# Graph-masked attention on one core: batches without a loop, and four places in the schedule moved

## The reference

```python
h = jnp.maximum(_layernorm(x, axis=-1), 0.0)
q = (h @ Wq + bq).reshape(b, n, H, HD)      # k and v in the same way
scores = jnp.einsum('bihd,bjhd->bhij', q, k) / jnp.sqrt(jnp.float32(HD))
scores = scores + jnp.where(adj == 0, -1e9, 0.0)[None, None, :, :]
weights = jax.nn.softmax(scores, axis=-1)
x = x + jnp.einsum('bhij,bjhd->bihd', weights, v).reshape(b, n, H * HD)
```

## Time and profile before

| | before |
|---|---|
| median of 3 runs | 4096.61 us (4095.68 to 4096.75) |
| the profiled execution | 4094.8 us, span of its instructions 4093.0 us |
| granted TensorE clock | 0.996 of full speed |
| busy: PE | 4027.1 us (98%) |
| busy: DVE, ACT, POOL | 76%, 75%, 34% |

### The profile page before, as it was taken

How to read it: one execution, slowest core, us unless ns; L and a number is a source line. 1 busy time by engine, 2 the same in 40 slices (tenths; PEclk the granted TensorE clock), 3 DMA queues, 4 the chain that set the end, 5 groups by cost and what they waited for, 6 DMA issues and landing times.

```text
span 4093.0 us, 77408 instructions
## 1 busy us (share of the span) xinstructions
PE 4027.1 (98%) x22016; PEld 3279.4 (80%) x22016; DVE 3100.4 (76%) x5128; ACT 3075.5 (75%) x5514; POOL 1394.2 (34%) x1409
## 2 busy tenths in 40 slices
PE   7999999999999999999999999999999999999998
PEld 6888888878887888878888788887888878888886
DVE  6877878777777777768777687776877868778686
ACT  5877868778686786867868688686886868868687
POOL 4333333333333333323333333332333333333322
PEclk9999999999999999999999999999999999999999
DMA  5232322322222222223222232222322323223121
GB/s 181 69 92 63 85 65 77 86 66 83 80 64 84 72 82 81 62 80 84 70 81 70 73 91 62 81 80 63 92 65 77 84 57 92 77 65 92 44 73 47
DMA packets 240106, 316.30 MB, mean 77 GB/s; under 512 B 16400, under 2 KB 147472, under 8 KB 231056
## 3 DMA queue, kind: packets, MB, share of 16 engines
q1 hardware_dynamic: 239632, 310.71, 26.6%
HBM read 172.23 MB, written 37.75 MB: 51 GB/s over the span
## 4 chain that ended last, share of the span: by engine, by line
PE 81%; issue 9%; POOL 5%; DMA 2%; ACT 2%; SPq 1%; DVE 0%; POOLq 0%; ACTq 0%; DVEq 0%
PE T L559 18%; PE misc L517 14%; PE S L547 10%; PE S L548 10%; PE O L571 10%; PE O L578 10%; PE misc L530 8%; DMA xln<-in_x 1%; POOL kB L400 1%; POOL kA L400 1%; PE misc L587 1%; PE misc L496 1%; POOL xln L381 1%; ACT y L670 1%; POOL outs L420 1%
## 5 line engine op out<-in xcount | busy, mean ns | idle before, releaser
L847 DVE TENSOR_TENSOR pT<-T,pT 128x512 fp32r<-128x512 f32 x2048 | 1390.7, 688 | 712.5 <-ACT pT L679 699.7
L679 ACT CAST pT<-T 128x512 fp32r<-128x512 f32 x2048 | 1185.5, 590 | 671.1 <-PE T L559 573.6
L841 DVE CUSTOM_DVE_ANT_0 S<-S,mask 128x1024 f32<-128x1024 f32 x1024 | 1257.2, 1228 | 9.0 <-PE S L548 8.1
L559 PE MATMUL T<-ident,probs 128*128 128x128 f32 x8192 | 1233.9, 273 | 0.6 <-DVE pT L847 0.2
L559 PEld LDWEIGHTS T<-ident,probs 128*128 128x128 f32 x8192 | 1005.1, 140 | 279.7 <-DVE pT L847 36.4
L687 ACT ACTIVATE probs<-S,negmax 128x1024 f32<-128x1024 f32 x1024 | 1151.6, 1125 | 8.3 <-DVE negmax L841 5.1
L578 PE MATMUL O<-pT,vs 128*64 128x512 f32 x2048 | 965.6, 471 | 0.2 <-DVE pT L847 0.2
L571 PE MATMUL O<-pT,vs 128*128 128x512 f32 x2048 | 816.9, 399 | 14.7 <-issue 14.6
L517 PE MATMUL misc<-hT,wqk 128*128 128x512 f32 x3036 | 789.7, 395 | 4.3 <-ACT y L670 0.8
L517 PEld LDWEIGHTS misc<-hT,wqk 128*128 128x128 f32 x3036 | 557.0, 188 | 156.5 <-ACT y L670 18.4
L420 POOL TENSOR_TENSOR outs<-outs,oT 64x512 f32<-64x512 f32 x256 | 331.7, 1296 | 560.8 <-DMA outs<-oT 539.7
(11 more groups left out here) (70 smaller groups left out, 3590.3 us busy)
## 6 DMA issues: line engine op xcount, KB each, us to landing
wqk<-wqk_split SPq DMA_DIRECT2D x63, 1024.0 KB, 6.5
xln<-in_x SPq DMA_DIRECT2D x240, 256.0 KB, 2.6
outs<-in_x SPq DMA_DIRECT2D x66, 512.0 KB, 4.5
kA<-kA SPq DMA_DIRECT2D x128, 256.0 KB, 3.2
kB<-kB SPq DMA_DIRECT2D x128, 256.0 KB, 3.9
outs<-oT SPq DMA_DIRECT2D x256, 128.0 KB, 3.4
out<-outs SPq DMA_DIRECT2D x64, 512.0 KB, 4.0
probs<-in_adj SPq DMA_DIRECT2D x4, 1024.0 KB, 5.0
```

Source lines behind the costliest of these rows:

```text
L559: mm = pe.transpose(T[:, u % 2, i * P:(i + 1) * P], probs[:, (GB * g + i) % RING, j * P:(j + 1) * P], ident[:])
L679: act.copy(pT[:, u % PT, 0, :], T[:, u % 2, :]).then_inc(p_hi, 1)
L841: dve.tensor_tensor_reduce(S[:, s % 2, :], S[:, s % 2, :], mask[:, s % NB, :], 1.0, 3.0e38, ALU.add, ALU.min, negmax[:, s % RING:s % RING ...
L847: dve.tensor_tensor(pT[:, u % PT, 1, :], T[:, u % 2, :], pT[:, u % PT, 0, :].bitcast(F32), ALU.subtract).then_inc(p_lo, 1)
```

## The change

There are four parts.
1. The loop is gone: every batch is written out on every engine, with constant counts. The semaphore increments dve_passed, gp_passed and sp_passed go with it.
2. The second q/k chunk moves from units (5, 6) to (6, 7) of a pair, and the low parts of q are given units of their own (LOW_AT).
3. On SP the load of an x tile stands ahead of copy_k in the same unit, and the second copy_k moves from unit 15 to 16 of a pair.
4. In the units 122, 124, 126 and 0 TensorE scores only the first half of the block; the second half comes in the odd unit after it, ahead of V. VectorE's shift moves to that odd unit.

```diff
-QK_SLOTS = ((3, 4), (5, 6), (8, 9), (11, 12))
+QK_SLOTS = ((3, 4), (6, 7), (8, 9), (11, 12))
...
-LOW_AFTER = (1, 3)
+LOW_AT = {8: (1, 0), 10: (1, 1), 11: (2, 0), 13: (2, 1)}
...
-COPY_K_AT, STORE_AT, RES_AT, WQK_AT = (8, 15), 19, 24, (21, 21, 28, 21)
+COPY_K_AT, STORE_AT, RES_AT, WQK_AT = (8, 16), 19, 24, (21, 21, 28, 21)
...
+HALVED = (122, 124, 126, 0)
...
-                    for half in range(2):
-                        if v == COPY_K_AT[half] and not (last and p == PAIRS - 1):
-                            copy_k(b, p + 1, half)
                     if u in HT_AT and HT_AT[u] + XLN < NB and not last:
                         t = HT_AT[u]
                         sp.wait_ge(h_turned, NB * (b + 1) + t + 1)
                         load_xln(b + 1, t + XLN)
+                    for half in range(2):
+                        if v == COPY_K_AT[half] and not (last and p == PAIRS - 1):
+                            copy_k(b, p + 1, half)
...
-            with sp.Fori(0, B // 2 - 1) as two:
-                body(2 * two + 1)
-                body(2 * two + 2)
+            for b in range(1, B - 1):
+                body(b)
...
-            def score(b, s):
+            def score(b, s, halves=(0, 1)):
...
-                for half in range(2):
+                for half in halves:
...
-                mm.then_inc(scored, 1)
+                if 1 in halves:
+                    mm.then_inc(scored, 1)
...
-                if u % 2 == 0 and s < SBLOCKS:
-                    score(b, s)
-                if u % 2 == 0 and s >= SBLOCKS and not last:
-                    score(b + 1, s - SBLOCKS)
+                halves = (u % 2,) if u // 2 * 2 in HALVED else (0, 1) if u % 2 == 0 else ()
+                if halves and s < SBLOCKS:
+                    score(b, s, halves)
+                if halves and s >= SBLOCKS and not last:
+                    score(b + 1, s - SBLOCKS, halves)
...
-                    if u % 2 == 0 and s < SBLOCKS:
+                    due = u % 2 == (1 if u // 2 * 2 in HALVED else 0)
+                    if due and s < SBLOCKS:
                         shift(b, s)
...
-                    for second in range(2):
-                        v = u - LOW_AFTER[second]
-                        if v in QK_AT and QK_AT[v][1] in Q_CHUNKS and not (last and QK_AT[v][0] == PAIRS - 1):
-                            low_q(b, QK_AT[v][0] + 1, QK_AT[v][1], second)
+                    if u % PER in LOW_AT and not (last and u // PER == PAIRS - 1):
+                        low_q(b, u // PER + 1, *LOW_AT[u % PER])
```

More of the change, by code:

```diff
@@ L177, in adj_preln_kernel @@
         o_turned, y_scaled, y_added = sem("o_turned"), sem("y_scaled"), sem("y_added")
-        dve_passed, gp_passed, sp_passed = sem("dve_passed"), sem("gp_passed"), sem("sp_passed")
         block = ctx.enter_context(nc.Block())
@@ L219, in load_xln @@
             def load_xln(b, t):
-                sp.sem_inc(sp_passed)
                 sp.dma_start(xln[:, t % XLN, :], x[b, t * P:(t + 1) * P, :]).then_inc(xln_in[t % XLN], 16)
             def load_xres(b, p):
-                sp.sem_inc(sp_passed)
                 src = x[b].rearrange("(i t) c -> t i c", t=P)[:, :, p * P:(p + 1) * P]
@@ L364, in spread @@
                 gp.wait_ge(mv_done, n + tiles)
-                gp.sem_inc(gp_passed)
                 gp.tensor_scalar(rstd[:, ts], mv[:, ts, 1], EPS, None, ALU.add).then_inc(ln_part, tiles)
@@ L478, in _ @@
             body(0, first=True)
-            with gp.Fori(0, B // 2 - 1) as two:
-                body(2 * two + 1)
-                body(2 * two + 2)
+            for b in range(1, B - 1):
+                body(b)
             body(B - 1, last=True)
@@ L539, in score @@
                 pair = PAIRS * b + s // 16
[L540 to L543, removed]
-                for half in range(2):
+                if 0 in halves:
+                    pe.wait_ge(q_low, 4 * pair + 3 + (s // 8) % 2)
+                    pe.wait_ge(k_copied, 64 * (pair + 1))
+                    if some(n - 1):
+                        pe.wait_ge(exped, n - 1)
+                for half in halves:
                     cols = slice(half * HALF, (half + 1) * HALF)
@@ L644, in _ @@
             body(0, first=True)
-            with pe.Fori(0, B // 2 - 1) as two:
-                body(2 * two + 1)
-                body(2 * two + 2)
+            for b in range(1, B - 1):
+                body(b)
             body(B - 1, last=True)
@@ L787, in _ @@
             body(0, first=True)
-            with act.Fori(0, B // 2 - 1) as two:
-                body(2 * two + 1)
-                body(2 * two + 2)
+            for b in range(1, B - 1):
+                body(b)
             body(B - 1, last=True)
@@ L806, in stats @@
                 dve.wait_ge(bn_done, n + 1)
-                dve.sem_inc(dve_passed)
                 dve.bn_aggr(mv[:, t, :], bn[:, r, :]).then_inc(mv_done, 1)
@@ L907, in body @@
                     s = u // 2 + LEAD
-                    if u % 2 == 0 and s < SBLOCKS:
+                    due = u % 2 == (1 if u // 2 * 2 in HALVED else 0)
+                    if due and s < SBLOCKS:
                         shift(b, s)
-                    if u % 2 == 0 and s >= SBLOCKS and not last:
+                    if due and s >= SBLOCKS and not last:
                         shift(b + 1, s - SBLOCKS)
@@ L921, in _ @@
             body(0, first=True)
-            with dve.Fori(0, B // 2 - 1) as two:
-                body(2 * two + 1)
-                body(2 * two + 2)
+            for b in range(1, B - 1):
+                body(b)
             body(B - 1, last=True)
```

## The result

The changed kernel takes 4112.09 us (median of 7 runs, 4110.31 to 4113.07) against 4096.61 us (7 runs, 4093.86 to 4097.57). The ratio is 1.0039, 95% interval 1.0027 to 1.0051: slower by 0.39%, 15.5 us, where 8.8 us less were forecast.

What follows compares the result with a forecast made beforehand. The prediction took TensorE, busy 98% of the span, as the bound, so only its waits could change. Its terms summed to -8.8 us, taking the median from 4096.6 to 4087.8 us, range 4076 to 4098.

Steps and rivals of the forecast that it cites:

- Part 2, unit 11: a new wait: Unit 11: qB moved to unit 9 delays ScalarE's copy_y, so chunk 3 waits 0.75 us, 62 times: +46.5 us.
- unit 11 costs less: Rival: the moved qB copy overlaps its neighbours (4073 us) or is hidden wholly (4041 us); chance 0.14.
- the bound that took no overlap: ScalarE, units 9 and 10: qB's copy and probs_hi overlap no neighbour, so probs_hi moves by 0.76 us.
- the six branches: Batch passages, unit 127 to unit 2: the branches back cost 4.1 us each and go, -24.8 us.
- waits that stay: Unit 3 of three pairs and unit 77: waits grow by 0.06 us without the loop in 14 batches, +3.4 us.
- x tile 3, unit 85: Unit 85: TensorE's wait for the tile's normalisation goes in 15 batches because its load is issued earlier, -12.7 us.
- V next to V: Units 125, 127 and 1: halved scores between consecutive V remove 0.22 us each, in 15 batches, -9.9 us.
- unit 5: Chunk 1 no longer starts right after chunk 0, so 63 waits of 0.18 us go, -11.3 us.
- Part 1, no loop: Batch passages take 12.03 us without a branch instead of 16.34: -24.8 us, with +3.4 us from waits that grow.
- a straight stream that runs dry: Rival: instruction fetch stalls TensorE 2.4 us each time; one in each of 14 batches gives 4121 us; chance 0.10.
- small waits: With the rival that the early load fails or a later tile waits, they leave 4092 to 4101 us; chance 0.12.

Runs made afterwards that it cites:

- a1_low12: The changed kernel with q's low part (2, 1) on VectorE back in unit 12 instead of 13: 4092.61 us, ratio 0.9991 to the kernel before.
- a2_qb8: The changed kernel with chunk 1's second high part (qB) on ScalarE in unit 8, right behind the first, instead of the end of unit 9: 4055.92 us.
- a3_swap: The changed kernel with chunk 1's halves exchanged: upper-partition qB made in unit 8, lower-partition qA at the end of unit 9: 4087.22 us.
- b1_noloop: The kernel before with only the loop removed, all batches written out: 4067.66 us, ratio 0.9938.
- b2_xload: The kernel before with only the x tile load put ahead of the copies of k and the second copy_k in unit 16: 4082.65 us, ratio 0.9968.
- b3_halves: The kernel before with only the scores halved next to V: 4083.39 us, ratio 0.9971.
- b4_qk: The kernel before, loop kept, with only chunk 1 moved to units 6 and 7 and the low parts' new table: 4150.06 us, ratio 1.0136.
- d2_low9: The changed kernel with copy_y ahead of the exponential, qB high in unit 8, low parts in units 8, 9, 11, 12: 4045.04 us, ratio 0.9882.
- d1_spread: d2_low9 with VectorE's statistics in units 5, 7, 9, 12, 37, 39, 41, 44 instead of 5, 7, 11, 13, 37, 39, 43, 45: 4015.66 us.

## Why the prediction was wrong

**The step that failed** is in "Part 2, unit 11: a new wait": "Behind it nothing else is late: VectorE and probs_hi of unit 10 have two units." It looked at VectorE behind unit 11 for what a later ScalarE would do to it. The table LOW_AT also moves VectorE's own low part (2, 1) from unit 12 to 13, and this move was never costed. It puts 0.69 us between probs_low and the next one, in a stretch in which probs_low was just in time. a1_low12 shows the price: its span is 19.3 us shorter, where the whole change had lost 18.3.

**The term of unit 11** was right in mechanism and place, and mis-sized: 0.90 us each instead of 0.75, 56 us instead of 46.5. The working had the copy itself and probs_hi behind it without overlap, but let the exponential follow as before. It doesn't; a2_qb8 and a3_swap give the sizes. The rival "unit 11 costs less" went the wrong way: the bound that took no overlap stopped one instruction short.

**The terms one by one.** The table has what each was forecast to bring and what it brought, in us: the distances between the starts of turn_probs, unit for unit, in the traces before and after, all 2048 of them.

| term | forecast | by the starts |
|---|---|---|
| the six branches | -24.8 | -24.5 |
| waits that stay | +3.4 | +3.6 |
| x tile 3, unit 85 | -12.7 | -13.5 |
| V next to V | -9.9 | -10.0 |
| unit 5 | -11.3 | -11.7 |
| unit 11 | +46.5 | +55.2 |
| unit 16 | none | +20.8 |
| all the rest | none | -1.6 |
| sum | -8.8 | +18.3 |

**What held.** "Part 1, no loop": the branches cost nothing any more and the passage is 12.07 us; the waits that stay are 0.41 each, as foretold, so the +3.4 stands. Its account of the 4.1 us was incomplete: the part that isn't the issue wait was put down to a staggered start and units running late, and in four of the six passages most of it is TensorE at half its clock (last section). The size held since it was taken from the starts. The other slower rival, a straight stream that runs dry, didn't come: no issue wait after, and b1_noloop gains. "Part 3, x tile 3" (-12.7; b2_xload's span -13.7) and "Part 4, V next to V" (-9.9; b3_halves -11.2) are right to 1.3 us. "Part 2, unit 5" is gone from the waits as forecast.

**The sum with both corrections** is -8.8 + 8.7 + 20.8 = +20.7 us, against +18.3 of span. Of the 2.4 between, 1.8 are four waits of scoring for copies of k, in units 22 and 54 of batches 6, 8 and 14, which the trace before has and the one after hasn't; the traces of b1_noloop and b4_qk haven't them either, so no one part removes them. The range ended at 4098 because its slow side held only the stream that runs dry and small waits. No row was read of what VectorE does in units 13 to 16, though the diff names 13.

## What to carry to other kernels

When a table moves work, every entry that moves is costed on its own engine, at its new neighbours, even where the change seems to be about another engine. Look above all at stretches where the bound engine has no filler work: there the helpers' instructions must be few, and two that were harmless apart cost 0.7 us together. An instruction moved ahead of another in one engine's order also moves that other one: copy_y ahead of the exponential removed waits of 19 us and made 27 elsewhere. And work taken from a late engine helps only behind the place where it waits: a low part that stood ahead of that place gave nothing when it was moved (d2_low9), statistics taken from behind it gave 29 us (d1_spread).

## What the hardware showed that was not expected

**Instructions of ScalarE don't overlap where the partitions change.** A 64-partition copy from and to the upper half starts 0.71 us after its predecessor of 0.69, probs_hi 0.64 after the copy of 0.62, the exponential 0.62 after probs_hi; with the lower half it is 0.59, 0.51 and 0.48. That the exponential is held too fits its bias negmax, read in the lower partitions when the last read of that memory was in the upper ones. Which operand does it was not taken apart. The Trainium skill, "VectorE: DVE Perf Modes", Two Vector instructions with no wait between them, states for VectorE that an instruction is held until the earlier ones have finished if an input starts in another group of 32 partitions than the last read of that memory, or its output in another than the last write. By that rule all three would be held behind qB and none behind qA; the two traces agree, but on ScalarE, of which the section doesn't speak.

**The branch back has no fixed price, and a part of it is TensorE's clock.** With the same loop and the same turns it cost 24.8 us over six times before and 15.3 in b4_qk, where only the order of chunk 1 and low parts inside the body differ. The granted clock (the third number from the end) in the 12 us around two of the branches before, the first and the second, and around one of b4_qk:

```profile
817.00:829.00 12.00, 9.56 (x39) 7.20 (x38) 3.36 (x5) 2.92 (x6) 2.02 (x2) 0.86 0.03 6
1324.00:1336.00 12.00, 8.68 (x41) 6.36 (x40) 3.55 (x6) 3.59 (x7) 1.77 (x2) 1.00 0.02 6
...
2370.00:2382.00 12.00, 9.57 (x45) 7.08 (x44) 3.96 (x6) 3.79 (x7) 2.38 (x3) 1.00 0.03 8
```

In four of the six passages before, it fell to half, the lower level (1.2 of 2.4 GHz), within 1.4 us of the end of an issue wait of 2.2 to 2.7 us; from 821 to 825 us it is 0.57 in the mean, and the scoring matmuls start 0.43 us apart instead of 0.23. After the other two issue waits, 2.8 and 2.2 us long, it didn't fall, and in b4_qk, where they are 0.7 to 1.4 us, it never did. The four passages lost 4.2 to 4.7 us each, the other two 3.9 and 3.3; there TensorE comes to V sooner and waits 0.56 us more for issue. The Trainium skill, "Runtime: NRT & Kernel Launch", Instruction fetch mechanics, has a taken branch stall on the fetch of its target where that lies outside the fetched window; that the issue waits go with the branch agrees, and their size (14.6 us in all before, 6.5 in b4_qk) varies by about as much as the whole forecast sum, for a reason that no run shows.
